# Two passes of look-ups over six tables, with the first tile's rows among them

## The reference

```python
e = jnp.stack([tbl_0[ids[:, 0]], tbl_1[ids[:, 1]], ..., tbl_38[ids[:, 38]]], axis=1)   # 2048 x 39 x 32
conv1 = jnp.einsum('bid,bjd,ijk->bkd', e, e, W1.reshape(39, 39, 128))
hidden1, final1 = conv1[:, :64, :], conv1[:, 64:, :]
conv2 = jnp.einsum('bid,bjd,ijk->bkd', e, hidden1, W2.reshape(39, 64, 128))
z = jnp.sum(jnp.concatenate([final1, conv2], axis=1), axis=2)
h = jnp.concatenate([z, dense_ctx], axis=1)
h = jnp.maximum(h @ W_top1 + b_top1, 0.0)
h = jnp.maximum(h @ W_top2 + b_top2, 0.0)
y = h @ W_top3
```

## Time and profile before

| | us |
|---|---|
| runs of before: median (lowest to highest) | 811.2 (807.7 to 817.63) |
| the profiled execution | 808.5 |
| its span | 806.6 |
| PE busy | 739.2 |
| DVE busy | 697.9 |
| ACT busy | 572.3 |
| POOL busy | 543.3 |

### The profile page before, as it was taken

The page is one execution under the profiler, slowest core; times in us unless marked ns, Lnnn a source line. Parts: engine busy times, 40 slices in busy tenths (PEclk is TensorE's granted clock), DMA queues, the critical chain, the costliest instruction groups (busy, mean ns, idle before and its releaser), DMA issues.

```text
span 806.6 us, 18279 instructions
## 1 busy us (share of the span) xinstructions
PE 739.2 (92%) x6938; PEld 431.1 (53%) x6938; DVE 697.9 (87%) x1142; ACT 572.3 (71%) x1535; POOL 543.3 (67%) x538
## 2 busy tenths in 40 slices
PE   2991787899999999999999999998999999999997
PEld 1660132375656565655556464655556565656576
DVE  6971986879999999899989898997999999999962
ACT  1330335768888888888887878786888888788883
POOL 6877777777777777777777777777777777700000
PEclk9995986899999999999999999999999999999999
DMA  6738878988898888989898889888898989888500
GB/s 194 233 66 221 241 189 235 254 244 250 253 235 248 239 257 232 262 237 247 228 255 244 243 240 242 241 235 243 232 252 237 252 234 265 248 252 249 158 2 2
DMA packets 135720, 179.32 MB, mean 222 GB/s; under 512 B 105304, under 2 KB 116518, under 8 KB 117648
## 3 DMA queue, kind: packets, MB, share of 16 engines
q1 hardware_dynamic: 111524, 166.84, 71.6%
q0 software_dynamic: 17088, 8.78, 6.6%
q10 hardware_dynamic: 7020, 2.52, 1.2%
HBM read 166.35 MB, written 16.71 MB: 227 GB/s over the span
## 4 chain that ended last, share of the span: by engine, by line
PE 29%; DVE 20%; DMA 20%; ACT 11%; SPq 8%; POOL 6%; issue 6%; ACTq 0%; DVEq 0%; POOLq 0%
DVE blocks L787 18%; DMA copies<-xt 16%; PE hidden L420 14%; SPq L350 7%; PE sums L473 6%; PE sums L447 6%; POOL emb L386 6%; ACT arena L636 5%; DMA xt<-emb 2%; DMA emb<-in_tbl,ids_tile 2%; ACT hid_high L605 2%; PE sums L478 2%; DVE turned L819 2%; ACT xdiag L624 2%; ACT hidden L613 1%
## 5 line engine op out<-in xcount | busy, mean ns | idle before, releaser
L386 POOL DMA_INDIRECT emb<-in_tbl,ids_tile x534 | 543.1, 1017 | 164.8 <-issue 112.5
L787 DVE TENSOR_TENSOR blocks<-copies 117x512 f32<-117x512 f32 x840 | 524.7, 693 | 75.5 <-DMA copies<-xt 59.7
L420 PE MATMUL hidden<-blocks,w_pairs 117*64 117x512 f32 x1792 | 434.6, 614 | 40.3 <-DVE blocks L787 38.4
L636 ACT ACTIVATE arena<-sums 64x480 f32<-64x480 f32 (+2 forms) x936 | 293.0, 313 | 138.6 <-PE sums L447 125.6
L420 PEld LDWEIGHTS hidden<-blocks,w_pairs 117*64 117x64 f32 x1792 | 152.1, 139 | 244.9 <-issue 105.5
L447 PEld LDWEIGHTS sums<-xdiag,turned 64*103 64x103 f32 x2000 | 101.5, 172 | 82.5 <-issue 46.1
L624 ACT ACTIVATE xdiag<-turned 32x468 f32<-32x468 f32 (+1 forms) x256 | 118.8, 464 | 25.7 <-DVE turned L763 22.6
L447 PE MATMUL sums<-xdiag,turned 64*103 64x78 f32 x2000 | 115.4, 262 | 3.3 <-ACT arena L636 2.2
L605 ACT ACTIVATE hid_high<-hidden 32x512 f32<-32x512 f32 x126 | 74.1, 588 | 11.6 <-PE hidden L420 9.7
L473 PE MATMUL sums<-arena,weights 128*64 128x128 f32 x1280 | 78.5, 279 | 0.0
L473 PEld LDWEIGHTS sums<-arena,weights 128*64 128x64 f32 x1280 | 71.1, 139 | 2.4
(11 more groups left out here) (50 smaller groups left out, 258.3 us busy)
## 6 DMA issues: line engine op xcount, KB each, us to landing
copies<-xt SPq DMA_DIRECT2D x448, 312.0 KB
emb<-in_tbl,ids_tile POOLq DMA_INDIRECT x534
xt<-emb SPq DMA_DIRECT2D x32, 152.0 KB
xt<-xt SPq DMA_DIRECT2D x16, 304.0 KB
xt<-emb SPq DMA_DIRECT2D x32, 104.0 KB
blocks<-hot_t SPq DMA_DIRECT2D x6, 512.0 KB, 6.1
xt<-emb SPq DMA_DIRECT2D x32, 56.0 KB
weights<-in_finals SPq DMA_DIRECT2D x1, 1728.0 KB
```

Source lines behind the costliest of these rows:

```text
L386: pool.indirect_dma_start(out=emb[u][:, f * D:(f + 1) * D], out_offset=None, in_=tables[f], in_offset=bass.IndirectOffsetOnAxis(ap=ids_til ...
L420: mm = nc.tensor.matmul(hidden[64 * c:64 * c + 64, k % 2, bank, :], w_pairs[0:ROWS, t, bank * HALF_HID:bank * HALF_HID + HID], blocks[0:RO ...
L636: op = nc.scalar.activation(out[:, :, cols].rearrange("p h (u b) -> p h u b", u=2), g[rows, i], ACT.Copy)
L787: op = nc.vector.tensor_tensor(blocks[0:ROWS, at + c, :], a[:, cols], b[:, cols], ALU.mult)
```

## The change

The 12 look-ups run in another order: first the first 1,024 samples of all six tables, then the last 1,024 (look-up j is of table j % 6). Tile 0 belongs to the first pass, whose look-ups now cover all 1,024 samples (before, the first 128 were left out), and ACT copies its rows straight into `emb[0]`; a new semaphore, `hot_first`, counts those copies. Tile 0 gathers 33 features. All six tables are loaded at once and stay. The indices come in 12 transfers of 256 KB, the kept rows are stored in two transfers of six tables each, by pass, and the loads of tiles 1 and 8 wait for them. The spill of tile 0 comes in one piece behind all index loads. In every tile the repeated rows (`xt<-xt`) are now copied before the wait for the last part's gathers. GpSimd no longer waits for look-ups.

```diff
 LOOKUPS = 2 * N_HOT
-INDICES = 4
-TABLES = 4
+ONES_BEFORE = list(itertools.accumulate([0] + HOT_C + HOT_C))
+INDICES = 8
+TABLES = 5
...
-COPIES_FREE = LOOKUPS - 8
-ONES_PLACE = [j % 3 if j < COPIES_FREE else 2 if j % 2 == 0 else 0 for j in range(LOOKUPS)]
+TURNED_FREE = LOOKUPS - 3
+ONES_PLACE = [j % 3 if j < LOOKUPS - 1 else 0 for j in range(LOOKUPS)]
...
                     part = PARTS[s]
-                    sp.wait_ge(gathered[u][s], 16 * gathers(tile, s))
+                    if s < len(PARTS) - 1:
+                        sp.wait_ge(gathered[u][s], 16 * gathers(tile, s))
                     if s == 0 and tile:
                         sp.wait_ge(hot_rows_loaded[u], 16 * hot_loads(tile))
+                    elif s == 0:
+                        sp.wait_ge(hot_first, N_HOT)
                     if s == len(PARTS) - 1:
                         sp.wait_ge(spilled_first[u], 16 * 2 * (p + 1))
                         sp.dma_start(xt[u, F:F + AGAIN, :, :].rearrange("f h n -> (f h n)").rearrange("(a b) -> a b", a=16),
                                      xt[u, 0:AGAIN, :, :].rearrange("f h n -> (f h n)").rearrange("(a b) -> a b", a=16)
                                      ).then_inc(spilled[u], 16)
+                        sp.wait_ge(gathered[u][s], 16 * gathers(tile, s))
...
-                elif chunk == 1:
-                    sp.wait_ge(hot_looked, COPIES_FREE)
-                elif v in (2, 3):
+                elif chunk == 1 or v in (2, 3):
                     sp.wait_ge(hot_looked, LOOKUPS)
...
-            for f in range(F):
-                if f >= AT_ONCE:
-                    pool.wait_ge(hot_looked, (f - AT_ONCE) // A_LOOKUP + 1)
+            for f in range(N_HOT, F):
                 gather(0, f)
             pool.wait_ge(ids_loaded[1], 16)
-            for at, f in enumerate(range(N_HOT, F)):
-                pool.wait_ge(hot_looked, (F - AT_ONCE + at) // A_LOOKUP + 1)
+            for f in range(N_HOT, F):
                 gather(1, f)
...
             def copy_rows(j):
-                n, h = j // 2, j % 2
+                n, h = j % N_HOT, j // N_HOT
                 act.wait_ge(hot_summed, j + 1)
-                if n >= 4 and n % 2 == 0 and h == 0:
-                    act.wait_ge(hot_kept[n // 2 % 2], 16 * (n // 4))
+                if h == 0:
+                    nc.scalar.activation(emb[0][:, n * D:(n + 1) * D], sums[:, j % 4, 0:D], ACT.Copy).then_inc(hot_first, 1)
                 skip = 0 if h else 1
...
             for j in range(LOOKUPS):
                 stage(j)
-                if j % 4 == 1 and j > 4:
-                    keep((j - 5) // 4)
+                if j == N_HOT + 1:
+                    keep(0)
                 if j:
                     copy_rows(j - 1)
-                if j % 2 == 0 and j // 2 + 3 < N_HOT:
-                    unpack(j // 2 + 3)
-                    if j // 2 + 5 < N_HOT:
-                        load_table(j // 2 + 5)
+                if j + 3 < N_HOT:
+                    unpack(j + 3)
             copy_rows(LOOKUPS - 1)
-            keep(KEPT - 1)
+            keep(1)
...
-                skip = 0 if h else P
                 at = 0 if HOT_C[n] == 8 else 8
                 for c in range(HOT_C[n]):
-                    nc.vector.tensor_scalar(hot_ones[j][:, c, skip:], hot_index[n][0:HOT_P, h * HALF_B + skip:(h + 1) * HALF_B],
+                    nc.vector.tensor_scalar(hot_ones[j][:, c, :], hot_index[j][0:HOT_P, :],
                                             row_number[0:HOT_P, at + c:at + c + 1], None, ALU.is_equal).then_inc(ones_ready, 1)
...
             for j in range(LOOKUPS):
                 indices_to_ones(j)
-                if j % 2 and j // 2 + 2 < N_HOT:
-                    split(j // 2 + 2)
+                if j + 2 < N_HOT:
+                    split(j + 2)
```

More of the change, by code:

```diff
@@ L138, in build @@
         y_col = sb("y_col", [P, TILES], F32)
-        rows = sb("rows", [P, 2, TILES, 2, D], F32)
+        rows = sb("rows", [P, 2, TILES // 2, N_HOT, D], F32)
         row_number = sb("row_number", [P, 18], F32)
@@ L176, in build @@
         hot_consts_loaded = sem("hot_consts_loaded")
-        hot_raw_loaded = [sem(f"hot_raw_loaded{n}") for n in range(2)]
+        hot_raw_loaded = [sem(f"hot_raw_loaded{n}") for n in range(N_HOT)]
         hot_unpacked = sem("hot_unpacked")
@@ L185, in build @@
         hot_copied = sem("hot_copied")
+        hot_first = sem("hot_first")
         hot_kept = [sem(f"hot_kept{m}") for m in range(2)]
@@ L258, in gathers @@
             part = PARTS[s]
-            each = part.stop - max(part.start, N_HOT)
-            return each * (tile // 2 + 1) if tile % 2 else part.stop - part.start + each * (tile // 2)
+            return (part.stop - max(part.start, N_HOT)) * (tile // 2 + 1)
         def hot_loads(tile):
@@ L290, in load_hot_rows @@
                     sp.wait_ge(spilled[u], 16 * SPILLS * (tile // 2))
-                else:
-                    for m in range(2):
-                        sp.wait_ge(hot_kept[m], 16 * ((KEPT + 1 - m) // 2))
+                if tile in (1, TILES // 2):
+                    sp.wait_ge(hot_kept[tile // (TILES // 2)], 16)
                 sp.dma_start(emb[u][:, 0:N_HOT * D], hot_kept_rows[tile]).then_inc(hot_rows_loaded[u], 16)
@@ L533, in look_up @@
                     for bank in range(BANKS):
-                        skip = P if j % 2 == 0 and bank == 0 else 0
-                        mm = nc.tensor.matmul(hidden[0:3 * D, j % 2, bank, skip:512], upper[n][:, c, :],
-                                              hot_ones[j][:, c, bank * 512 + skip:(bank + 1) * 512],
+                        mm = nc.tensor.matmul(hidden[0:3 * D, j % 2, bank, :], upper[n][:, c, :],
+                                              hot_ones[j][:, c, bank * 512:(bank + 1) * 512],
                                               start=(c == 0), stop=(c == HOT_C[n] - 1))
@@ L543, in add_parts @@
                     pe.wait_ge(hot_copied, j - 3)
-                for t in range(0 if j % 2 else 1, TILES // 2):
+                for t in range(TILES // 2):
                     mm = nc.tensor.matmul(sums[:, j % 4, t * D:(t + 1) * D], staged[j % 2][:, t * P:(t + 1) * P],
```

90 lines of the change are left out of this document (41 added, 49 removed).

## The result

| | runs | us, median (lowest to highest) |
|---|---|---|
| before | 20 | 811.99 (807.7 to 818.8) |
| changed | 20 | 816.91 (811.0 to 823.05) |

The ratio is 1.0074, with a 95% interval of 1.0052 to 1.0095: 4 to 8 us slower, a small loss that the repeated runs do tell from nothing. The profiled execution of the changed kernel took 815.67 us, its span 813.9; that of before 808.5 and 806.6. So there are 7.3 us to be found.

A forecast was written before the change was run, and what follows sets the result against it. GpSimd's gathers were taken as the pacemaker, PE close behind: 8.4 us saved less 0.9 gives 7.5, so 808.5 - 7.5 = 801.0, plus 1 us towards the runs' median makes 802, with a range of 794 to 811.

The forecast's parts named there:

- part 5: GpSimd's gathers beside the longer stretch of one-hots: four gathers delayed by 0.22 us, 0.9 us lost, leaving 7.5 us gained.
- gathers of more than 1.3 us in the look-ups: Sign to look for in the changed profile: gathers growing beyond 1.3 us during the look-ups would show part 5 wrong.
- A first copy later than 62: Sign at the start: the first copy of `x`, forecast at 58, coming after 62 us would break part 2 or Part 3.
- part 2: Look-ups at the start: the first tile needs the sixth look-up, its rows ready at 48.5 us; last look-up ends at 66.1.
- Part 3: Spill of the first tile on SyncE: first copy of `x` starts at 58.1 in place of 65.50, 7.4 us earlier.
- GpSimd stands still beside the one-hots: Rival, chance 0.05: GpSimd blocked through the added 5.9 us of one-hots, gain only 2.5 us, 806.0.
- part 6: Repeated rows copied before the wait for each tile's last gathers: about half a microsecond once, counted as nothing.
- Part 1: First tile's gathers on GpSimd: six fewer, the 33rd issued at 49.72 us, path 8.40 us shorter.
- Part 4: Work no longer hidden at the start: second store of kept rows costs up to 3.6 us, second tile's copies 3.8 earlier.
- the rival that the ramp decides: Rival, chance 0.20: the middle does not make good what the second store takes at the start; gain 3.8 us, 804.7.
- The sum's last step: Whole kernel: PE's 10.5 us of waits in the middle shrink, so the end follows GpSimd's gathers, 808.5 - 7.5 = 801.0.
- The rival of the lower clock: Rival, chance 0.04: look-ups run at TensorE's lower clock, 1.2 GHz, and the start gets slower: 841, or 825 with half.

The follow-up runs named there:

- e6_self_wait: The changed kernel, with DVE waiting for its own last one-hot before every fourth one-hot: 800.56 us, ratio 0.9835 to the kernel before.
- e8_before_self_wait: The kernel before, with its 39 gathers, and DVE waiting for its own last one-hot before every fourth one-hot: 809.51 us, ratio 1.0004.
- e1_gap: The changed kernel, with each look-up's one-hots waiting for the end of the look-up two before: 805.66 us, ratio 0.9919 to the changed kernel.

## Why the prediction was wrong

**The step that failed is in part 5.** It read the earlier trace rows, a median of 1163 ns and a longest of 2072 ns beside the one-hots, as "a delay and not a standstill", and priced the longer stretch of one-hots with the mean delay: four gathers times 0.22 us, 0.9 us. The median was right for most gathers: those ahead of the held one took 1.68 and less. But the rows gave the wrong quantity. What decides is the longest run of one-hots without a pause, and one gather can lose all of it that is left when it starts: 19.49 us where a run is 22 us long, 4.45 where it is 6.6, at most 1.68 where it is 3.5 or less. The longest gather of before, 2.07, was that term already, kept small by the splits and by the waits for a free place. It ended at 27.70, and the one-hots beside it at 27.58 (POOL's and DVE's timelines of before):

```profile
25.63 2.07 POOL L386 DMA_INDIRECT emb<-in_tbl,ids_tile  x1 [0.30 <-issue]
24.33 3.25 DVE L866 TENSOR_SCALAR arena<-blocks,row_number 125x1024 bf16<-125x1024 int16 x8
```

The prediction had named the sign that came, gathers of more than 1.3 us in the look-ups. A first copy later than 62 came, too, but it did not mean part 2 or 3.

The Trainium skill, "SBUF — State Buffer", section "Who interferes with whom", which part 5 set aside, says that beside DVE in a two-port mode the second of the two engines is blocked fully and not slowed down. The runs agree with that for the gather that is caught: in all the traces together, 20 gathers beside the look-ups took over 1.6 us, and each ended 0.12 us behind the last one-hot of a run (those above at 55.66, 40.14, 45.95, 55.79 and 54.42). They do not agree with a block of one instruction only, since one gather sat through 49 one-hots of 0.4 us; nor with a block of every gather, since most pass with 0.3 us more.

**The rival had the place and not the price.** *GpSimd stands still beside the one-hots* had 0.05 and a gain of 2.5 us, because it let POOL stand still only during the added 5.9 us. The change adds more than length: with three places for one-hots to the end and the splits all done by 33.4, it takes away DVE's pauses for the whole of 33 to 55 us. Part 2 had the facts for that: "one after each of the first four look-ups' one-hots", and from there "TensorE sets the pace". That DVE, with three places, would run ahead of TensorE and so lose its waits was not worked out. On the path to the first copy the loss adds up so: 18.55 for the hold (19.49 less 0.94), less the 8.40 of the six gathers, less 1.74 since the others went a little quicker (the 33rd would stand at 47.98, not 49.72), plus 0.20 for the last one's travel (2.44, before 2.24), less 0.61 for the copy of repeated rows that no longer stands behind it (part 6), less 0.72 from the last spill's issue to the first copy (3.79, before 4.51): 7.28 us.

**Part 1 was right in size.** With the hold away, the 33rd gather began at 47.46 (`e6_self_wait`), where 49.72 was forecast. The four sets of such runs gained 0.7 to 1.65% against before, 6 to 13 us; the forecast was 7.5. They have the pauses as well as the six gathers less, and `e8_before_self_wait`, which was to tell the two apart, does not.

**Part 2 was right**: the sixth row was forecast for 48.5 and came at 48.8 (SyncE's issue at 48.90); the last look-up was to end at 66.1 and did, and PE's next wait begins at 67.5, as forecast. There was some luck in the end: the fifth look-up began 1 us late (36.69), and the rest followed at 3.68 us each, not 3.83. **Part 3** was near: with the hold away, the first copy starts at 58.9 to 60.2 in the three runs with short pauses, where 58.1 was forecast, and PE waits 2.8 to 4.3 us for it, where at most 3 was.

**Part 4 was wrong, without bearing on the sign.** The second store was put at 3.6 us of the ramp. In the changed kernel it had landed at 71.9, before the first copy; in the paused version it went beside the copies, which were no slower for it. So the rival that the ramp decides by it loses its ground.

**Part 6 was right**: it took 0.6 us out of the first tile's path, and by itself changed nothing within 0.5%.

**The sum's last step** was half right. The end of the changed kernel follows POOL's last gather (+7.1) and the first copy of `x` (+7.3) nearly one to one. But PE's wait for DVE in the middle did not shrink or grow: 10.6 us where the earlier trace rows had 10.5 (waits of 155 to 700 us):

```profile
PE hidden L415 <- DVE blocks L776: 10.6, 32, 1.7
```

With the hold away POOL did run ahead: in the traces of the three runs with short pauses the last gather came 6.6 to 9.5 us earlier than before, the end of the span 3.7 to 7.6, and PE's wait was 8.1 to 10.2 us. So the end kept part of POOL's lead or all of it, and the wait shrank by 2.4 us at most.

The rival of the lower clock falls: TensorE's granted clock was 1.00 from 14 to 56 us in the changed kernel, and the look-ups behind the first (6.19 us) took 3.63 us each.

**Open.** Which gather of a run is caught, and why most pass. In the changed kernel the one at 34.59 passed inside the run in 1.28 us, before the next was held; a port that both engines want is the Trainium skill's reading in the same section, and no run here shows the port or DVE's mode. The stores' and the clock's part in the spread of the paused versions, 794 to 810 us, was not taken apart.

## What to carry to other kernels

When a change gives an engine more buffers or removes its waits, list the pauses that it loses and ask who was served in them; here GpSimd's gathers lived on DVE's waits. Read the longest instruction of a group beside the median, and set its end against the other engines' pauses. A wait of a tenth of a microsecond, placed on purpose, was worth 12 to 19 us against the changed kernel here (ratios to the kernel before of 0.9835 to 0.9927, and of 1.0074 without it).

## What the runs showed of the hardware that was not expected

- One gather's issue stayed on GpSimd for 19.49 us beside 49 one-hots (16-bit in, 16-bit out, 0.4 us each). The kind of DVE work matters: beside f32 products without a pause (from 91.53 for 17.50 us) the gathers of 95 to 115 us kept their length, in the changed kernel:

```profile
91.53 17.50 DVE L776 TENSOR_TENSOR blocks<-copies 117x512 f32<-117x512 f32 x28
```

```profile
L384 POOL DMA_INDIRECT emb<-in_tbl,ids_tile x16: 940/944/1442, 94.6 to 113.5; - x16
```

Whether it is the operation, the type or the number of inputs, no run separates. One gather of `e1_gap` took 4.99 us beside such products, at 518.21; its cause was not looked for.

- DVE's wait for its own last result is pause enough: with one in each look-up no gather took over 1.67 us, though it lengthens a look-up's one-hots by only 0.1 to 0.5 us.
- A store on ScalarE's queue among SyncE's copies is slow itself and holds up whoever waits for it: 768 KB landed after 23.8 us (`e6_self_wait`), against 3.9 ahead of the copies in the changed kernel; 480 KB took some 18 us (`e8_before_self_wait`), against 4.7. The copies beside it moved no less in the one pair of traces compared. The loads of weights (1728 and 1028 KB), issued by SyncE behind the copies and ahead of tile 1's spill, made tile 1's first copy 9.4 us later (one run).
